# Column sums of the attention weights by four narrow fp32 matmuls, with the chain of the reciprocal one key tile later

## What is computed

```python
q = shape(hidden_states @ wq)
k = shape(hidden_states @ wk)
v = shape(hidden_states @ wv)
scores = jnp.einsum('bhqd,bhkd->bhqk', q, k)
scores = scores + position_bias
attn = jax.nn.softmax(scores.astype(jnp.float32), axis=-1).astype(scores.dtype)
out = jnp.einsum('bhqk,bhkd->bhqd', attn, v)
out = out.transpose(0, 2, 1, 3).reshape(b, s, INNER)
return out @ wo
```

## Time and profile before

| | us |
|---|---|
| median of three runs | 2945.34 |
| lowest and highest of them | 2944.24, 2945.95 |
| the profiled execution | 2945.1 |
| its span, first to last instruction | 2943.3 |
| PE busy | 2811.5 (96%) |
| POOL busy | 2414.9 (82%) |
| DVE busy | 1769.3 (60%) |
| ACT busy | 1663.7 (57%) |

### The profile page before, as it was taken

The page is one execution under the profiler, slowest core; times in us unless marked ns, Lnnn a source line. Parts: engine busy times, 40 slices in busy tenths (PEclk is TensorE's granted clock), DMA queues, the critical chain, the costliest instruction groups (busy, mean ns, idle before and its releaser), DMA issues.

```text
span 2943.3 us, 49274 instructions
## 1 busy us (share of the span) xinstructions
PE 2811.5 (96%) x18720; PEld 1043.8 (35%) x18720; DVE 1769.3 (60%) x4532; ACT 1663.7 (57%) x2117; POOL 2414.9 (82%) x1098
## 2 busy tenths in 40 slices
PE   5999999999999999999999999999999999977897
PEld 2333333333333333333333333333333333322443
DVE  7556555565655556655655566655656565584666
ACT  4555565555555555555555555556555655556576
POOL 0789999999989998999989899999999898988000
PEclk9999999999999999999999999999999999999999
DMA  5000000000000000000000000000000000101001
GB/s 159 26 5 9 9 26 9 5 8 13 21 9 5 9 26 9 9 5 26 9 9 9 5 26 9 8 9 23 8 9 8 9 12 9 65 8 33 4 1 58
DMA packets 48256, 52.69 MB, mean 18 GB/s; under 512 B 16482, under 2 KB 38114, under 8 KB 48018
## 3 DMA queue, kind: packets, MB, share of 16 engines
q1 hardware_dynamic: 48018, 49.52, 5.6%
HBM read 44.57 MB, written 10.82 MB: 19 GB/s over the span
## 4 chain that ended last, share of the span: by engine, by line
PE 58%; issue 18%; DVE 17%; POOL 4%; ACT 3%; DMA 0%; SPq 0%; DVEq 0%; ACTq 0%; POOLq 0%
PE po L635 20%; PE st L605 19%; PE pre L617 6%; PE pm L572 4%; POOL acc L540 4%; PE st L860 3%; DVE mpart L1311 3%; DVE pre L1303 2%; DVE st L1328 2%; PE pm L578 2%; DVE pre L1308 2%; PE pm L659 2%; PE pm L644 1%; DVE y L1350 1%; DVE mpart L1303 1%
## 5 line engine op out<-in xcount | busy, mean ns | idle before, releaser
L540 POOL TENSOR_TENSOR acc<-acc,prob 128x1024 f32<-128x1024 f32 x896 | 2115.2, 2361 | 222.4 <-ACT prob L948 133.9
L948 ACT ACTIVATE prob<-st 128x1024 f32<-128x1024 f32 x1024 | 1016.0, 1021 | 902.3 <-DVE st L1328 823.5
L635 PE MATMUL po<-prob,v 128*64 128x512 f32 x4096 | 994.5, 606 | 0.0
L605 PE MATMUL st<-qk 64*128 64x512 f16 x6144 | 835.0, 378 | 6.9 <-ACT prob L948 4.9
L1303 DVE CUSTOM_DVE_ANT_0 pre<-pre,ew 128x512 f32<-128x512 f32 x448 | 300.6, 712 | 562.0 <-issue 561.9
L1308 DVE CUSTOM_DVE_ANT_0 pre<-pre,tab 128x512 f32<-128x512 f32 x704 | 475.2, 715 | 150.8 <-issue 150.7
L605 PEld LDWEIGHTS st<-qk 64*128 64x128 f16 x6144 | 294.1, 94 | 329.6 <-ACT prob L948 43.3
L635 PEld LDWEIGHTS po<-prob,v 128*64 128x64 f32 x4096 | 249.0, 136 | 447.5 <-issue 374.0
L605 PE MATMUL st<-eq,ek 64*128 64x512 f16 x2048 | 390.0, 377 | 0.0
L617 PE MATMUL pre<-qk 64*128 64x512 f16 x1600 | 310.1, 384 | 42.1 <-ACT ew L978 18.9
L1311 DVE TENSOR_REDUCE mpart<-pre 128x2 f32<-128x1024 f32 x224 | 271.4, 1211 | 115.7 <-PE pre L617 114.9
(11 more groups left out here) (199 smaller groups left out, 2369.3 us busy)
## 6 DMA issues: line engine op xcount, KB each, us to landing
inv_b<-inv_scratch SPq DMA_DIRECT2D x130, 128.0 KB, 2.9
t_scratch<-w_scratch SPq DMA_DIRECT2D x2, 2688.0 KB
qk<-x SPq DMA_DIRECT2D x8, 512.0 KB, 5.5
out<-qk SPq DMA_DIRECT2D x8, 512.0 KB, 3.5
w<-w_pairs SPq DMA_DIRECT2D x8, 384.0 KB, 3.7
t2f<-t_scratch SPq DMA_DIRECT2D x8, 384.0 KB, 4.6
t<-t_scratch SPq DMA_DIRECT2D x8, 384.0 KB, 3.3
den_c<-den_s SPq DMA_DIRECT2D x130, 2.0 KB, 1.7
```

The lines of the kernel that those rows point to most:

```text
L540: nc.gpsimd.tensor_tensor(acc[g % 2][:, :, :], a, prob[:, n % RING, :, :], ALU.add).then_inc(sum_p, 1)
L605: last = nc.tensor.matmul(st[:, 2 * (n % 2) + h, :], w[64 * h:64 * h + 64, :], t[64 * h:64 * h + 64, :], start=(r == 0), stop=(r == len(te ...
L635: last = nc.tensor.matmul(po[64 * h:64 * h + 64, :], v[:, g // CHUNKS, j, 64 * h:64 * h + 64], prob[:, n % RING, h, :], start=(s == 0), st ...
L948: nc.scalar.activation(prob[:, n % RING, :, :], st[:, 2 * (n % 2):2 * (n % 2) + 2, :], ACT.Exp).then_inc(exp_done, 1)
```

## The change

The sums over the partitions are made by four matmuls with 32 columns each in place of two with 64. Matmul k takes head k // 2 and half k % 2 of its queries: 256 queries instead of 512. It writes partitions 32k to 32k + 31 and the first 256 columns of the bank. The copy out of PSUM is half as wide, and the sums are carried to `den_c` by four transfers of 16 partitions in place of two of 32.

Besides, four entries of the order are one step larger: the reciprocal (`INV_AT`), the normalisation (`NORM_AT`), the high half (`HIGH_AT`) and the low half (`LOW_AT`). The output stays at steps 12 and 14.

```diff
-INV_AT, NORM_AT, HIGH_AT, LOW_AT = 3, 7, 9, 10
+INV_AT, NORM_AT, HIGH_AT, LOW_AT = 4, 8, 10, 11
...
-        den_s = sb("den_s", [128, QC], f32)
+        den_s = sb("den_s", [128, QC // 2], f32)
...
-        unit = sb("unit", [128, 64], f32)
+        unit = sb("unit", [128, 32], f32)
...
-                for h in range(2):
-                    sp.dma_start(den_c[32 * h:32 * h + 32, :], den_s[64 * h:64 * h + 1, :].rearrange("o (a b) -> o a b", b=SQ)).then_inc(den_in, 16)
+                for k in range(4):
+                    sp.dma_start(den_c[SQ * k:SQ * k + SQ, :], den_s[32 * k:32 * k + 1, :].rearrange("o (a b) -> o a b", b=SQ)).then_inc(den_in, 16)
...
-                for h in range(2):
-                    last = nc.tensor.matmul(pm[64 * h:64 * h + 64, :], unit[:, :], acc[(g + 1) % 2][:, h, :], start=True, stop=True)
+                for k in range(4):
+                    h, half = divmod(k, 2)
+                    last = nc.tensor.matmul(pm[32 * k:32 * k + 32, 0:QC // 2], unit[:, :],
+                                            acc[(g + 1) % 2][:, h, QC // 2 * half:QC // 2 * half + QC // 2], start=True, stop=True)
                 last.then_inc(den_ready, 1)
...
-                    act.wait_ge(den_in, 32 * G)
-                nc.scalar.activation(den_s[:, :], pm[:, :], ACT.Copy).then_inc(den_row, 1)
+                    act.wait_ge(den_in, 64 * G)
+                nc.scalar.activation(den_s[:, :], pm[:, 0:QC // 2], ACT.Copy).then_inc(den_row, 1)
...
-                dve.wait_ge(den_in, 32 * (G + 1))
+                dve.wait_ge(den_in, 64 * (G + 1))
```

## The result

The changed kernel takes 2972.57 us (median of four, 2971.07 to 2974.68) against 2944.84 for the kernel before, run beside it: a ratio of 1.0095, 95% interval 1.008 to 1.011. It is slower by 27.7 us, where I had forecast 18.9. The profiled execution has a span of 2971.3 us.

What follows compares the result with a forecast made beforehand. PE was taken as the bound, busy 322.95 of 326.15 us. Terms summed to 2.2 us lost per pair, 15.4 for seven pairs, plus 3.5 for the last: 18.9 on 2945.1, so 2964 us, range 2947 to 2990.

Steps and rivals of the forecast that it cites:

- 2953 to 2976: Whole kernel: the span given to the prediction's own forecast of 2964 us by itself, chance 0.50.
- the last pair: Eighth pair: round g = 4 already waits for POOL, its low half would end 2.3 us later; 3.5 us lost.
- Part 1: Sums on PE: four narrow matmuls run together and the copy shrinks, saving 2.53 us of PE per pair.
- 0.43 us per sums: Sums on PE: two half passes instead of two full ones save 0.43 us, in full in five rounds of eight.
- a change of form is paid twice: Rival, sums on PE: 32 columns cost a second 0.11 us in 48 to 64 rounds, giving 2970 us; chance 0.12.
- Part 2: Reciprocal on DVE a step later: leaves a chain PE waits for, 0.155 us in four rounds, 0.62 per pair.
- POOL has lead enough: POOL's normalisation: the later reciprocal shrinks its lead by 0.8 us in g = 0; no loss was counted.
- Part 3: High half on ACT a step later: delays the Relu PE waits for, 0.54 us in g = 0, 1, 2, 4, 5, 6.
- never rests: POOL in the short rounds without projections, g = 3 and 7: said to have no idle time.
- Part 4: Low half on POOL behind one more sum: PE's output 1.16 us later in g = 3, 0.70 in g = 7, net.
- DVE's 1.46 us and 2.48 us: DVE in g = 1 and 3: times for wo's low half and the weight split, limiting the matmuls' saving to 0.15 and 0.
- the rival of losses that are made good: Rival, whole kernel: engines running ahead while PE is held remove later waits, half the loss returns, 2948 us; chance 0.09.

Runs made afterwards that it cites:

- narrow_inv: The changed kernel with the old order except the reciprocal, which stays a step later (4, 7, 9, 10): 2936.34 us, ratio 0.9972.
- High_alone: The changed kernel with the old order except the high half, which stays a step later (3, 7, 10, 10): 2976.15 us, ratio 1.0107.
- low_alone: The changed kernel with the old order except the low half, which stays behind one more addition (3, 7, 9, 11): 2945.34 us, ratio 1.0004.
- Small_wl: The changed kernel with DVE's low half of the weights cut from 768 columns to 96 in all pairs but the first: 2966.98 us.
- after_splits_moved: The changed kernel with DVE's two low halves of weights moved behind additions of y, and ACT's high halves moved too: 2960.5 us, ratio 1.0052.

## Why the prediction was right, and where its sizes were off

The direction and the range held: 2972.6 lies between 2947 and 2990, with slower at 0.79. It lies even in the narrower 2953 to 2976 of my forecast, but with luck: with the last pair as forecast it would have been about 2977, and a gain there that I had not foreseen brought it back. The size was short, 18.9 against 27.7 us, by several steps.

- **Part 1, the four matmuls.** Right that all four run together, and the copy of 0.38 us was forecast at 0.37. The term of 0.43 us per sums was too large: it is 0.29, since a change of form is paid twice. This was a rival, priced at 0.11 us and given a chance of 0.12; it costs 0.12 to 0.13. The rows already showed 0.11 us for leaving one form, and I set the second aside because weights could be loaded ahead. That makes 0.14 us in each of five rounds, 0.7 us a pair.
- **Part 2, the reciprocal.** Right in kind, 0.10 us in place of 0.155. That POOL has lead enough was right only together with the later normalisation: narrow_inv lost it.
- **Part 3, the high half.** The 0.54 us is confirmed by 0.52 in g = 2 and 6. In g = 0 it is 0.66, with a wait of 0.62 us for the Relu; I have no cause for the difference. What failed is that I followed the high half to PE through the Relu and not to POOL, which waits for it too: it was a wait that the order shows (the low half stands behind it), and I had checked only that the low half came in time for the output. High_alone shows what hangs on it: 3.0 us a pair in g = 3 and 7. In the changed kernel POOL's delay costs g = 3 0.37 us over low_alone, and more in g = 1 (below). I had also written that POOL "never rests" in g = 3 and 7; in g = 3 it is busy for 34.35 of 37.28 us, waits up to 0.81 us for single exponentials in the first steps, and only then stands back to back.
- **Part 4, the low half.** 1.16 and 0.93 us before the saving of part 1 (0.70 + 0.23) were forecast for g = 3 and 7; low_alone lost 1.31 and 1.12. In the changed kernel PE does wait there for the low half, 0.75 and 0.39 us, after 0.53 and 0.68 for the Relu. But these are no terms of their own, since the high half alone brings g = 3 to +1.74 and g = 7 to +1.09.
- **g = 1 and g = 3.** The forecast took DVE's 1.46 us and 2.48 us as durations. They are waits for the most part. Small_wl gives 0.70 of the 1.69 us of g = 3 back by cutting the operation's own work. Moving both away gives 1.2 us in g = 3 and 0.5 to 0.8 in g = 1.
- **The last pair.** The step that failed is that a late start of g = 4 stays lost: 3.5 us forecast, -0.25 measured. Most of what g = 4 did lose, 1.64 of 1.99 us, was a fallen clock, which no term had. I had not looked at g = 5 and 6, where PE waits for DVE and ACT for several us. Here the rival of losses that are made good was true, in one pair of eight.

Per pair, the misses are 0.33 us in g = 0, 0.43 in g = 1, 0.53 in g = 3, 0.22 in g = 7 and 0.12 to 0.19 in each of the other four, 2.1 us in all for the third pair. Seven pairs together lost 29.1 us and not 15.4, so 13.7 too little; the last pair is 3.7 too much. The first sums also start 0.9 us earlier than before. 18.9 + 13.7 - 3.7 - 0.9 is 28.0, which is the difference of the two spans.

## What to carry to other kernels

When a step on one engine is moved, follow every engine that waits for its result, not just the one that you think is the bound: here the loss ran through POOL as well as through the Relu. Compare the shortest and the longest run of an instruction before taking its mean as a cost: one that takes 0.95 us once and 2.48 us seven times is waiting inside its own row, and its place in time, not its size, is what to change. A faster part and a worse order can come in one change; measured apart they gave -11 and +41 us. The faster part, with the later reciprocal and normalisation and with two operations of DVE and ACT's work for them moved, gave -26. What these moves give without the narrow matmuls was not run.

## What the runs showed of the hardware

- A DVE operation with both inputs in SBUF that starts during one of POOL's additions (SBUF to SBUF) does not end before that addition does, whatever its size: 2.15 us for 96 columns, 2.84 for 768. A time of its own comes on top: 0.82 us for 768 columns, 0.28 for 256, 0.12 for 96. By themselves the first two take 0.95 and 0.41 us. A multiplication and addition of constants on 16 columns, with a single input in SBUF, took 2.26 us in the last pair, and 0.17 where POOL was idle. If DVE starts first, POOL's addition is lengthened: 2.61 against 2.36 us for 256 columns, and 2.88 where the 768 columns had themselves been waiting. Additions of y, with one input in PSUM, kept 0.68 to 0.69 us beside POOL all the time.
- Four fp32 blocks of 32 columns run at once, with the pass of 256 rows at 0.24 us: the sums take 0.58 us in place of 0.97 for two blocks of 64 columns with 512 rows.
- Going from 64 to 32 columns costs PE 0.10 us, and 0.12 to 0.13 with what follows in each round with projections; in all 5.3 us.
- Behind a wait of PE at the output the granted clock fell to 0.50 (1.2 GHz) for 2 to 3 us in some rounds and not in others with the same wait: after 1.12 us in g = 3 of the third pair of after_splits_moved, and not after 1.13 to 1.15 us in five other pairs. A fall costs about 1.6 us.
- The chain from the reciprocal through two transfers back to SBUF takes 5.3 to 7.4 us in the rounds of narrow_inv where POOL waits for it.
